# Paired score tiles and one 1024-column exponential in the first attention; the bank rings become two pairs and two singles

## The reference, cut to what matters

```python
h = (x - mu) * rsqrt(var + LN_EPS) * ln_scale + ln_bias
c_q = h @ w_down_q.T;  c_kv = h @ w_down_kv.T
q, k, v = per-head up-projections of c_q, c_kv, c_kv      # 16 heads of 64
q = rope(q);  k = rope(k)
scores = einsum('bhqd,bhkd->bhqk', q, k) / 8
attn = softmax(scores, axis=-1)
out = einsum('bhqk,bhkd->bhqd', attn, v) @ w_out.T + residual
```

## Time and profile before

| what | value |
|---|---|
| median of 3 runs | 2269.47 us (2269.19 to 2272.49) |
| span of the profiled execution | 2374.5 us |
| first attention's steps in it, first to last | 61.5 to 1317.5 us |
| PE, DVE, ACT, POOL busy in those 1256 us | 1236.77, 1058.63, 1124.07, 1212.44 us |
| granted TensorE clock in them | 1.00 |

### The profile page before, as it was taken

The page is one execution under the profiler, slowest core; times in us unless marked ns, Lnnn a source line. Parts: engine busy times, 40 slices in busy tenths (PEclk is TensorE's granted clock), DMA queues, the critical chain, the costliest instruction groups (busy, mean ns, idle before and its releaser), DMA issues. The chain is left out here.

```text
span 2374.5 us, 61611 instructions
## 1 busy us (share of the span) xinstructions
PE 2104.0 (89%) x24894; PEld 1370.7 (58%) x24894; DVE 1848.8 (78%) x3743; ACT 1681.0 (71%) x3414; POOL 1695.7 (71%) x1103
## 2 busy tenths in 40 slices
PE   5899999999999999999999799766687877777788
PEld 1466666666666666666666466423465655555565
DVE  7788888888888888888885589786789887567324
ACT  4898988988988989889899466565465554443343
POOL 4899999999999999999999366355433345555400
PEclk9999999999999999999999899786789988776578
DMA  4000000000000000000000001111121111111101
GB/s 146 1 2 2 2 2 2 2 2 2 2 2 2 2 2 2 2 2 2 2 2 2 15 25 34 42 25 33 32 46 32 42 35 29 27 32 29 25 14 36
DMA packets 57653, 44.07 MB, mean 19 GB/s; under 512 B 34896, under 2 KB 47776, under 8 KB 57120
## 3 DMA queue, kind: packets, MB, share of 16 engines
q1 hardware_dynamic: 45856, 28.38, 4.4%
q0 software_dynamic: 11520, 11.82, 2.5%
HBM read 34.35 MB, written 1.61 MB: 15 GB/s over the span
## 5 line engine op out<-in xcount | busy, mean ns | idle before, releaser
L380 POOL TENSOR_TENSOR probs_lo<-probs,probs_hi 128x1024 f16<-128x1024 f32 x512 | 1076.3, 2125 | 43.1 <-ACT probs L430 42.6
L494 DVE TENSOR_REDUCE part_max<-aux 128x1 f32<-128x512 f32 x1024 | 677.6, 686 | 91.2 <-PE aux L568 86.8
L429 ACT ACTIVATE probs_hi<-scores 128x512 f16<-128x512 f32 x1024 | 630.2, 615 | 134.8 <-PE scores L601 117.5
L430 ACT ACTIVATE probs<-scores 128x512 f32<-128x512 f32 x1024 | 636.6, 622 | 0.0
L1693 POOL DMA_INDIRECT far<-key_table,placeT x320 | 319.6, 999 | 343.3 <-PE a_turn L1944 75.8
L617 PE MATMUL acc<-v,probs_hi 128*128 128x65 f16 x4096 | 451.1, 193 | 2.3 <-POOL probs_lo L380 2.3
L619 PE MATMUL acc<-v,probs_hi 128*128 128x64 f16 x4096 | 452.3, 195 | 0.0
L621 PE MATMUL acc<-v,probs_lo 128*128 128x65 f16 x4096 | 450.5, 192 | 0.0
L617 PEld LDWEIGHTS acc<-v,probs_hi 128*128 128x128 f16 x4096 | 382.5, 96 | 82.6 <-POOL probs_lo L380 2.5
L619 PEld LDWEIGHTS acc<-v,probs_hi 128*128 128x128 f16 x4096 | 380.0, 97 | 75.5
L568 PE MATMUL aux<-k_a,q_a 128*128 128x512 f16 x1024 | 390.8, 382 | 6.4 <-DVE roped L480 2.1
(11 more groups left out here) (333 smaller groups left out, 4101.6 us busy)
## 6 DMA issues: line engine op xcount, KB each, us to landing
far<-key_table,placeT POOLq DMA_INDIRECT x360
qT<-qT SPq DMA_DIRECT2D x16, 256.0 KB
queries<-places SPq DMA_DIRECT2D x7, 512.0 KB
e_w<-in_e_w SPq DMA_DIRECT2D x48, 64.0 KB, 1.9
near_value<-key_table SPq DMA_DIRECT2D x128, 12.0 KB
x<-in_x SPq DMA_DIRECT2D x4, 256.0 KB, 3.7
cos<-in_cos SPq DMA_DIRECT2D x1, 1024.0 KB, 7.2
sin<-in_sin SPq DMA_DIRECT2D x1, 1024.0 KB, 9.2
```

What stands on the lines that cost most here:

```text
L380: pool.tensor_tensor(probs_lo[:, slot], probs[:, wide], probs_hi[:, slot], ALU.subtract).then_inc(low_ready, 1)
L429: act.activation(probs_hi[:, slot, i], bank, ACT.Exp, scale=float(DH0) ** -0.5)
L430: act.activation(probs[:, wide, i], bank, ACT.Exp, scale=float(DH0) ** -0.5).then_inc(probs_ready, 1)
L494: dve.tensor_reduce(part_max[g % 2][:, n % QT, n // QT:n // QT + 1], bank, AX.X, ALU.max).then_inc(aux_free, 1)
```

## The change

Scores get two tiles of two neighbouring banks each (`[P, 2, CH]`, `SCORES = 2`, four banks), and the `aux` ring shrinks from three banks to two (`AUX = 2`); `acc` keeps two. Both score tiles of a step go into one pair. PE waits for a free pair once a step and signals once, after the second tile. ACT takes one fp16 and one fp32 exponential of 1024 columns, where it took two of each of 512. POOL waits for the same moment as before, counted in steps.

```diff
--- before.py
+++ after.py
@@ -283,8 +283,8 @@
 LAG = 4
 SLOTS = 5
 WIDE = 3
-SCORES = 3
-AUX = 3
+SCORES = 2
+AUX = 2
 ROPED = 4
 QRING = 4
 WEIGHTS_AT = -19
@@ -341,7 +341,7 @@
         inv = [sb(f"inv{i}", [P, QT], F32) for i in range(2)]
         heads_out = sb("heads_out", [P, NT, 2, DH0], F32)
         headsT = sb("headsT", [P, CH], F32)
-        scores = [ps(f"scores{i}", [P, CH], F32) for i in range(SCORES)]
+        scores = [ps(f"scores{i}", [P, 2, CH], F32) for i in range(SCORES)]
         acc = [ps(f"acc{i}", [P, CH], F32) for i in range(2)]
         aux = [ps(f"aux{i}", [P, CH], F32) for i in range(AUX)]
         (aux_full, aux_free, rope_turned, hi_ready, lo_ready, shift_ready, scores_ready, probs_ready, low_ready,
@@ -376,7 +376,7 @@
 
                 def low_half(n):
                     slot, wide = n % SLOTS, n % WIDE
-                    pool.wait_ge(probs_ready, 2 * n + 2)
+                    pool.wait_ge(probs_ready, n + 1)
                     pool.tensor_tensor(probs_lo[:, slot], probs[:, wide], probs_hi[:, slot], ALU.subtract
                                        ).then_inc(low_ready, 1)
 
@@ -422,12 +422,10 @@
                         act.wait_ge(probs_used, n - SLOTS + 1)
                     if n >= WIDE:
                         act.wait_ge(low_ready, n - WIDE + 1)
-                    for i in range(2):
-                        tile = 2 * n + i
-                        bank = scores[tile % SCORES][:]
-                        act.wait_ge(scores_ready, tile + 1)
-                        act.activation(probs_hi[:, slot, i], bank, ACT.Exp, scale=float(DH0) ** -0.5)
-                        act.activation(probs[:, wide, i], bank, ACT.Exp, scale=float(DH0) ** -0.5).then_inc(probs_ready, 1)
+                    banks = scores[n % SCORES][:]
+                    act.wait_ge(scores_ready, n + 1)
+                    act.activation(probs_hi[:, slot], banks, ACT.Exp, scale=float(DH0) ** -0.5)
+                    act.activation(probs[:, wide], banks, ACT.Exp, scale=float(DH0) ** -0.5).then_inc(probs_ready, 1)
 
                 def weight_half(i):
                     w = keep[WEIGHTS[i]]
@@ -588,18 +586,19 @@
 
                 def score(n, i):
 
-                    g, h, tile = n // KPAIR, n // STEPS, 2 * n + i
+                    g, h = n // KPAIR, n // STEPS
                     if n % KPAIR == 0 and i == 0:
                         pe.wait_ge(lo_ready, rope_no["q", h, g % NCH] + 1)
                         pe.wait_ge(aux_free, unit_no["shift", g] + 1)
-                    if tile >= SCORES:
-                        pe.wait_ge(probs_ready, tile - SCORES + 1)
+                    if n >= SCORES and i == 0:
+                        pe.wait_ge(probs_ready, n - SCORES + 1)
                     key = 2 * (n % KPAIR) + i
                     keys = slice(key * P, (key + 1) * P)
-                    out = scores[tile % SCORES][:]
+                    out = scores[n % SCORES][:, i, :]
                     pe.matmul(out, ka[h % 2][:, keys], qa[g % QRING][:], start=True, stop=False)
-                    pe.matmul(out, kb[h % 2][:, keys], qb[g % QRING][:], start=False, stop=True
-                              ).then_inc(scores_ready, 1)
+                    ins = pe.matmul(out, kb[h % 2][:, keys], qb[g % QRING][:], start=False, stop=True)
+                    if i:
+                        ins.then_inc(scores_ready, 1)
 
                 def weigh(n, i):
```

## The result

The changed kernel takes 2345.98 us (median of four runs), the kernel before 2269.33; the ratio is 1.0342, with a 95% interval of 1.031 to 1.0373. One of the four runs took 3341.74 us at a granted clock of 0.552 and is left out of the ratio, but not of the median; the others took 2340.77, 2342.6 and 2349.36.

What follows compares the result with a forecast made beforehand. It took PE's own stream as the bound, with POOL close behind: 86.9 us of late fills less 10 us of PE's old waits gave +77 us on 2269.5, so 2346 us, range 2322 to 2378.

Steps and rivals of the forecast that it cites:

- The later start on pairs: ACT starts 0.44 us later, on the second tile, and `probs` completes 0.35 us later; costed at nothing.
- q's rope: PE's second maximum after q's rope chunks waits for DVE: 0.69 us twice and 0.33 us twice a head.
- the shift: The fill at a shift waits for DVE's maxima around a block's normalisation: 0.78 us, three times a head.
- the second `v`: Next head's second `v` unit, straight behind k's last rope: PE waits 1.19 us for DVE, once a head.
- late fills: PE's waits to fill `aux` until DVE empties the unit two before: 5.79 us a head, 86.9 us in 15 heads.
- the first `v`: First of the next head's two `v` units: PE waits 0.22 us for DVE, once a head.
- PE's old waits: PE's present waits for ACT, bounds 6.4 and 26.0 us; 10 us of them were taken to go.
- The profiled span of 2451: Forecast for a profiled execution of the changed kernel: the earlier span of 2374.5 plus 77 us.
- A spare third bank: Rival: the third `aux` bank was spare, only PE's waits for ACT change; 2259 us, faster; 5 in 100.
- Shorter waits than counted: Rival: one wait moves a head's later clusters, so half the waits vanish; 2303 us; 8 in 100 for 2290 to 2322.
- ACT or POOL as the bound: Rival: dearer two-bank exponentials, or 0.35 us repeating on POOL each step (+59 more, 2405 us); 2 in 100.
- The clock did not fall: Rival: PE's pauses lower the granted clock in the attention to 0.93, 95 us more, 2441 us; 7 in 100.

Runs made afterwards that it cites:

- e5: The changed kernel with its pairs and ring of two, but each pair read by four exponentials of 512 columns; 2347.72 us.
- e2: The kernel before with four single score banks, an `aux` ring of two and exponentials of 512 columns; 2351.1 us.
- e10: The kernel before, with three single score banks, given an `aux` ring of two and another order of the units (ropes, normalisation, transposition, output product moved); 2278.3 us.
- e1: The kernel before with only the `aux` ring cut from three banks to two, three single score banks kept; 2354.97 us.
- e9: The changed kernel with DVE's sine product written to a new SBUF tile, so the rope sum reads only SBUF and the bank frees sooner; 2753.13 us.

## Why the prediction was right, point by point

**PE is the bound, ACT is covered: right.** Four short exponentials took 54 us of ACT's idle time and moved the stage by 1.9 us (e5), and all groups show engines that wait longer for PE. The 1024-column exponential takes 1.02 us and the next starts 751.63 - 750.71 = 0.92 later, as I had worked it out from one that reads SBUF (1.06 us); reading across two banks is no dearer than that. In the timeline of after:

```profile
750.71 1.02 ACT L427 ACTIVATE probs_hi<-scores 128x1024 f16<-128x1024 f32 x1 [0.75 <-PE scores L599]
751.63 1.02 ACT L428 ACTIVATE probs<-scores 128x1024 f32<-128x1024 f32 x1
```

**The later start on pairs costs nothing: right.** e2 and e10 have singles in place of pairs and the same time within some 5 us. The waits for a free pair are fewer than the waits for a free single bank were.

**The ring of two is the cost: right, and shown alone by e1.** The places are those of the account. Behind q's rope in head 8, where it had PE late by 0.69 us: DVE's sum ends at 740.65 + 0.69 = 741.34, PE's second maximum starts 0.05 later.

```profile
740.65 0.69 DVE L478 TENSOR_TENSOR roped<-aux,rope_term 128x512 f32<-128x512 f32 x1
...
741.39 0.39 PE L566 MATMUL aux<-k_a,q_a 128*128 128x512 f16 x1 [0.37 <-DVE roped L478]
```

At the shift of the same head: the maximum two units back ends at 751.84 + 0.68 = 752.52, the fill starts at 752.57.

```profile
751.84 0.68 DVE L492 TENSOR_REDUCE part_max<-aux 128x1 f32<-128x512 f32 x1
...
752.57 0.39 PE L566 MATMUL aux<-k_a,q_a 128*128 128x512 f16 x1 [0.27 <-DVE part_max L492]
```

And behind the second `v`: 792.92 + 0.69 = 793.61, and 793.67. Of the 1.19 us counted there, this fill pays 0.22 and the one before it, behind k's last rope (791.60 + 0.69 = 792.29, and 792.35), 0.95. Two units on, a fill waits once more, by 0.44 us, for a maximum behind the normalisation of a block (794.76 + 0.68 = 795.44, and 795.49).

```profile
791.60 0.69 DVE L478 TENSOR_TENSOR roped<-aux,rope_term 128x512 f32<-128x512 f32 x1
...
792.35 0.39 PE L566 MATMUL aux<-k_a,q_a 128*128 128x512 f16 x1 [0.79 <-DVE roped L478]
...
792.92 0.69 DVE L488 TENSOR_TENSOR v<-aux,v 128x512 f16<-128x512 f32 x1
...
793.67 0.39 PE L566 MATMUL aux<-k_a,q_a 128*128 128x512 f16 x1
...
794.76 0.68 DVE L492 TENSOR_REDUCE part_max<-aux 128x1 f32<-128x512 f32 x1
...
795.49 0.39 PE L566 MATMUL aux<-k_a,q_a 128*128 128x512 f16 x1 [0.28 <-DVE part_max L492]
```

**The sum: its total right, its two terms off by some 5 and 6 us, and these errors cancel by luck.** The 86.9 us for late fills measured 92.0 (93.4 less the 1.4 of before). The shifts counted (0.33 + 0.44 us each, paid at two fills), q's ropes and the first `v` came out as worked out. What is missing is the fourth shift of each head, behind the second `v`: I let the largest lateness of that cluster, 1.19 us, stand for all of it, and the 0.44 of the normalisation came on top, 6.6 us in 15 heads. "About ten places a head" were 15, since one lateness is often paid at two fills in a row.

The 10 us that I let PE's old waits give back measured 16.4. Only 5.7 came from the waits for ACT, which I had named, and not for the reason that I gave, a PE slowed by the ring: with the ring of two and three single banks (e1) late scores stayed at 10.5 of 11.4 us, and they fell with four score banks, paired or single (e2). The other 10.7 came from the shifts' waits for the reduced maxima, which I had not named: PE now arrives at the fourth shift of a head later, because of the waits just ahead of it, and finds it ready.

That the forecast of 2346 met the median of 2345.98 so closely is luck as well: the three runs that the ratio uses have a median of 2342.6.

**The profiled span of 2451: wrong.** It was 2340.8. I carried the 105 us of the profiled execution of before along; they lay behind the attention and did not come back. The forecast for the median did not depend on it.

**The rivals.** A spare third bank falls with e1. Shorter waits than counted fall with the 92.0 us. ACT or POOL as the bound falls with e5 and with POOL's idle time of 120.5 us. The clock did not fall: 1.00 over the stage with waits of up to 1.1 us for a bank. The rule of the Trainium skill that I set beside it ("TensorE: Matmul & The Clock Gate", "A second HAM failure mode: psum-queue depth-cycling") did not hold for pauses of this length here. In e9, with waits of up to 6.5 us, the stage's mean clock was 0.89 (a mix of 2.4 and 1.2 GHz), so a lower clock did come with much longer pauses for a bank; whether shorter ones than these ever cost clock, no run here shows:

```profile
PEld aux L567 <- DVE part_max L493: 177.4, 132, 6.5
...
65.00:1800.00 1735.00, 1397.46 (x16906) 862.82 (x16905) 1380.80 (x1741) 1080.21 (x1222) 1233.88 (x635) 0.89 0.01 1
```

## What to carry to other kernels

In this kernel the ring between the engine that sets the pace and a helper that is idle a sixth of the time was not sized by that share but by the longest thing that the helper does between two hand-overs. To price a smaller ring, compare, place by place, the pacing engine's start with the helper's end one buffer fewer back; the latenesses of the repeating pattern add up to the price, and two of them that stand close together may both count. The same list shows which instructions to move; here another order of the units gave back 75 of the stage's 77 us with the smaller ring, and one number of it made the old kernel 0.4% faster. Making instructions of a covered engine longer and fewer moves only its idle time.

## What the runs showed of the hardware

A VectorE sum of two fp32 SBUF operands, 128x512, took 0.69 us at the least, but where it met a run of back-to-back GpSimd instructions it mostly ended only after the whole run. In e9, the row of the line, then DVE's and POOL's timeline at one place:

```profile
L479 DVE TENSOR_TENSOR roped<-rope_other,rope_term x128: 691/2162/7266, 31.7 to 1739.1; 128x512 f32<-128x512 f32 x128
...
264.92 5.80 DVE L479 TENSOR_TENSOR roped<-rope_other,rope_term 128x512 f32<-128x512 f32 x1
...
263.88 6.28 POOL L381 TENSOR_TENSOR probs_lo<-probs,probs_hi 128x1024 f16<-128x1024 f32 x3
```

The sum starts 1.04 us into the first of three subtractions, ends at 270.72, and the third of them ended at 270.16. It was not served between them. Of the 128 sums, 59 waited in this way over two to four GpSimd instructions in a row until GpSimd fell idle, and 33 over a single one after which it was idle; they ended about 0.55 us behind it. But 18 were served between two GpSimd instructions in a row, of which the later then took 0.4 to 0.5 us longer than usual; what decides between the two outcomes is not shown. The other 18 started while GpSimd was idle. With one operand in PSUM the same sum took 0.69 us beside the same GpSimd work, in the changed kernel:

```profile
L478 DVE TENSOR_TENSOR roped<-aux,rope_term 128x512 f32<-128x512 f32 x128 | 88.6, 692 | 17.7 <-DVE aux L473 1.0
```

The Trainium skill, "SBUF — State Buffer", section "Who interferes with whom", says that a VectorE instruction with two SBUF inputs contends with a GpSimd instruction that reads SBUF, and that the one that comes second waits. The trace agrees for the first of the three subtractions; the other two came after the sum and went ahead of it all the same.
